# A selective-scan layer on one core: half of a GpSimd product, a mask product, a gate job, a low-part copy and a carry handover move to other tiles

## The reference, cut to what matters

```python
xr, gate = split(x @ W_in.T, 2)              # x: 2 sequences x 2048 steps x 512
xr = xr + t_emb
xc = silu(causal_conv4(xr) + b_conv)         # depthwise, 1024 channels
xn = layernorm(xc) * ln_g + ln_b
Bm, Cm, dt = split(xn @ W_xproj.T, 3)        # 16 states each
dt = tanh(dt @ W_dt.T + b_dt) * 0.01
Ad = 1.0 + dt * A
Bd = Bm * minimum(norm(xn), 1.0)
h  = clip(h * ad[:, :, None] + bd[:, :, None] * xt[:, None, :], -10, 10)   # scan over the steps
yt = einsum('bd,bdh->bh', ct, h)
y  = ys + D * xn                             # the "D product"
out = x + (y * silu(gate)) @ W_out.T
```

## Time and profile before

| | before |
|---|---|
| median of 3 executions | 2055.43 us (2054.57 to 2057.09) |
| profiled execution, its own time | 2052.24 us |
| span of the profiled execution | 2050.5 us |
| TensorE matmul busy | 1826.6 us, 89% |
| GpSimd busy | 1753.4 us, 86% |
| VectorE busy | 1637.6 us, 80% |
| ScalarE busy | 1376.2 us, 67% |

### The profile page before, as it was taken

How to read it: one execution, slowest core, us unless ns; L and a number is a source line. 1 busy time by engine, 2 the same in 40 slices (tenths; PEclk the granted TensorE clock), 3 DMA queues, 4 the chain that set the end, 5 groups by cost and what they waited for, 6 DMA issues and landing times.

```text
span 2050.5 us, 46002 instructions
## 1 busy us (share of the span) xinstructions
PE 1826.6 (89%) x16240; PEld 1396.0 (68%) x16240; DVE 1637.6 (80%) x2109; ACT 1376.2 (67%) x3462; POOL 1753.4 (86%) x1476
## 2 busy tenths in 40 slices
PE   5689998899999899999898999899999899899888
PEld 4466776676776676676676777676677676677655
DVE  3478887888887888888887888788888788888786
ACT  5577666777666776766676766676766677766643
POOL 1489988889988889988889988889988889988886
PEclk9799999999999999999999999999999999999999
DMA  5222222222222222222222222222222222222221
GB/s 178 58 69 54 70 58 74 63 78 59 67 58 75 62 79 59 67 57 77 62 77 59 67 63 71 62 75 59 69 72 62 64 73 61 67 75 58 62 67 29
DMA packets 168069, 139.14 MB, mean 68 GB/s; under 512 B 100704, under 2 KB 137968, under 8 KB 163168
## 3 DMA queue, kind: packets, MB, share of 16 engines
q1 hardware_dynamic: 167840, 136.20, 24.9%
HBM read 62.07 MB, written 9.31 MB: 35 GB/s over the span
## 4 chain that ended last, share of the span: by engine, by line
PE 29%; POOL 25%; issue 19%; ACT 15%; DVE 8%; SPq 2%; DMA 1%; POOLq 0%; DVEq 0%; ACTq 0%
POOL prod L1094 17%; PE ps_y L590 6%; ACT tap L750 5%; PE ps_job L517 5%; PE ps_job L483 4%; DVE ks L995 4%; PE ps_fill L573 3%; PE ps_fill L564 3%; ACT low L793 3%; PE ps_job L496 2%; POOL xn L1039 2%; POOL xn L1042 2%; PE ps_job L490 2%; SPq L406 1%; ACT xh L688 1%
## 5 line engine op out<-in xcount | busy, mean ns | idle before, releaser
L1094 POOL TENSOR_TENSOR prod<-ks,crep 128x512 f32<-128x512 f32 x1024 | 1286.0, 1274 | 142.1 <-DVE ks L995 140.4
L995 DVE TENSOR_TENSOR_SCAN ks<-low,ps_fill 128x512 f32<-128x512 f32 x1024 | 1208.3, 1208 | 227.0 <-PE ps_fill L573 226.7
L793 ACT COPY low<-ps_fill 128x512 f32<-128x512 f32 x1024 | 584.6, 580 | 477.0 <-PE ps_fill L564 474.4
L590 PE MATMUL ps_y<-c_sb,prod 128*128 128x128 f32 x4096 | 613.4, 275 | 9.9 <-ACT xc L758 7.1
L590 PEld LDWEIGHTS ps_y<-c_sb,prod 128*128 128x128 f32 x4096 | 457.5, 142 | 75.9 <-issue 27.1
L573 PE MATMUL ps_fill<-spans,pick 128*128 128x512 f16 x1024 | 390.7, 381 | 76.4 <-ACT low L793 71.8
L564 PEld LDWEIGHTS ps_fill<-ts,xs 128*128 128x128 f16 x4096 | 315.8, 98 | 171.8 <-issue 10.7
L564 PE MATMUL ps_fill<-ts,xs 128*128 128x128 f16 x4096 | 397.9, 220 | 9.2 <-DMA xs<-h 7.6
L750 ACT ACTIVATE tap<-xr,cols_sb 128x128 f32<-128x128 f32 x768 | 251.9, 393 | 0.0
L478 PE MATMUL ps_job<-x,w_in 128*128 128x128 f16 x3072 | 215.9, 221 | 10.3 <-POOL x L1064 7.8
L483 PE MATMUL ps_job<-w_in,x 128*128 128x512 f16 x768 | 202.0, 379 | 21.3 <-ACT gate L682 21.3
(11 more groups left out here) (124 smaller groups left out, 1962.7 us busy)
## 6 DMA issues: line engine op xcount, KB each, us to landing
crep<-c_dram SPq DMA_DIRECT2D x32, 1024.0 KB, 4.7
xs<-xh SPq DMA_DIRECT2D x256, 64.0 KB, 2.0
xs<-xl SPq DMA_DIRECT2D x224, 64.0 KB, 2.0
xf<-in_xT SPq DMA_DIRECT2D x32, 256.0 KB, 2.8
res<-in_x SPq DMA_DIRECT2D x32, 256.0 KB, 2.8
out_dram<-res SPq DMA_DIRECT2D x32, 256.0 KB, 2.3
ts<-tth SPq DMA_DIRECT2D x128, 32.0 KB
ts<-tth SPq DMA_DIRECT2D x128, 31.0 KB
```

The lines of the kernel that those rows point to most:

```text
L590: last = mm(ps_y[:, cut], prod[:, (TILES * k + s) % HOLD, e, :], ident, start=False, stop=(u % 4 == 3 and q == 3 and e == QN - 1), is_tran ...
L793: copy(low[:, (TILES * k + s) % RING], ps_fill[:, (TILES * k + s) % RING]).then_inc(sem["low_copied"], 1)
L995: nc.vector.tensor_tensor_scan(ks[:, u % 2, QN * q:QN * (q + 1)].rearrange("d n t -> d (n t)"), low[:, g % RING], ps_fill[:, g % RING], 0. ...
L1094: tt(prod[:, g % HOLD], ks[:, u % 2, part], crep[:, p, part], ALU.mult).then_inc(sem["weighed"], 1)
```

## The change

Six things move; no arithmetic is added or taken out.
1. The second gate job goes from points 8 to 11 to points 9 to 12, and its take from 12 to 13.
2. The second half of the D product goes from tile 11 to tile 22, with the wait for the transposed y of the chunk before.
3. The second mask product (`ttl`) goes from tile 18 to tile 21.
4. `bqm`'s low part goes from point 27 to 29.
5. In the carries ScalarE makes the fp16 copy at TAKE and copies the 16 rows into `lend` one point later, behind a wait for VectorE's low part; VectorE no longer waits for `lend_set`. The bank of a carry counts as free at `lend_set`.
6. The taps move from points 24, 28, 30, 34, 38, 40, 43, 46 to 24, 28, 33, 38, 40, 42, 44, 47.

```diff
-                (7, 1, "yT", 1, -1, 2, 1), (8, 4, "gate", 1, 0, 2, 0),
+                (7, 1, "yT", 1, -1, 2, 1), (9, 4, "gate", 1, 0, 2, 0),
...
-        TAKE = {("z", 0): 5, ("gate", 0): 7, ("hend", 0): 6, ("yT", 1): 8, ("gate", 1): 12,
+        TAKE = {("z", 0): 5, ("gate", 0): 7, ("hend", 0): 6, ("yT", 1): 8, ("gate", 1): 13,
...
-        TAP_AT = [24, 28, 30, 34, 38, 40, 43, 46]
+        TAP_AT = [24, 28, 33, 38, 40, 42, 44, 47]
...
-                    pe.wait_ge(sem[name + "_taken"], (kk + off) * per + i + 1)
+                    freed = "lend_set" if name == "carry" else name + "_taken"
+                    pe.wait_ge(sem[freed], (kk + off) * per + i + 1)
...
                     copy(ch[:, half], bank("carry", i)).then_inc(sem["carry16"], 1)
+                for i in range(2):
+                    if point != TAKE["carry", i] + 1 or not exists(k, 1):
+                        continue
+                    half = slice(i * BANK, (i + 1) * BANK)
+                    act.wait_ge(sem["carry_taken"], 2 * (k + 1) + i + 1)
                     if exists(k, 0):
                         act.wait_ge(sem[f"lend_in{p}"], 16 * pair(k, p, 0))
                     copy(lend[:, half], bank("carry", i)[0:NS]).then_inc(sem["lend_set"], 1)
-                if point == 27 and exists(k, 1):
+                if point == 29 and exists(k, 1):
...
-                    dve.wait_ge(sem["lend_set"], 2 * j + i + 1)
...
                         pool.wait_ge(sem["xn_done"], k + 1)
+                        skipped(p, 0)
+                    if s == 22 and exists(k, 0):
                         since(pool, "yT_in1", N_YT * k)
-                        for i in range(2):
-                            half = slice(i * BANK, (i + 1) * BANK)
-                            tt(xd[i], xn[:, p, half], row_d[:, half], ALU.mult).then_inc(sem["xd_done"], 1)
+                        skipped(p, 1)
...
-                    if s in (14, 18) and exists(k, 1):
-                        h = s // 4 - 3
+                    if s in (14, 21) and exists(k, 1):
+                        h = s // 21
...
+            def skipped(p, i):
+
+                half = slice(i * BANK, (i + 1) * BANK)
+                tt(xd[i], xn[:, p, half], row_d[:, half], ALU.mult).then_inc(sem["xd_done"], 1)
```

## The result

The changed kernel takes 2126.24 us (median of four executions, 2120.06 to 2130.53) against 2055.0 us for the kernel before (median of four; the 2055.43 above is that of three): the ratio is 1.0346, 95% interval 1.0317 to 1.0375. Forecast were 2115 us, 2080 to 2136.

A forecast was written before the change was run, and what follows sets the result against it. No engine alone was the bound; the copies behind `ttl` would bind. Waits of 53.7 (steady), 3.9 and 2.4 us, together 60, on 2052.24 make 2112; the median, 3.2 above, gives 2115 us, range 2080 to 2136.

The forecast's parts named there:

- The chain from `ttl` to the fill: GpSimd's `ttl`, SyncE's 18 copies, then the next chunk's tile 0 fill: 15.1 us to the landing, 2.5 us of room.
- `ttl` 5.2 us later, 2.7 over the room: At tile 21 `ttl` ends 5.2 us later; with 2.5 us of room the fill waits 2.7 us a pass, less G.
- The sum: 29 steady passes at 1.85 us make 53.7, pass 0 adds 3.9 and pass 30 adds 2.4: together 60 us.
- G: How much earlier the other moves bring the scan of tile 21: 0.25 (gate) + 0.6 (carries) = 0.85 us a pass.
- D product worth nothing in a steady pass: Moving its second half takes 1.27 us from GpSimd's full stretch before tile 21, but gains nothing in a steady pass.
- The taps cost nothing here: First conv take comes about 0.8 us later, but TensorE awaits it ahead of a fill already late: no cost.
- The page's 2.0 us: Fixed cost of a DMA; by it room is 4.0 us, the wait 1.2 less G, some 10 us over 29 passes.
- The three waits: The waits that the edits name, 1.77, 2.21 and 0.78 us; the faster rival had them go nearly in full.
- the faster one: Rival: scan of tile 21 over 2.7 us earlier, copies land in time, pass 0.55 us shorter, 2038 us; chance 0.05.
- The rival that ScalarE is the bound: Copies not the bound; the late conv take costs 0.8 - 0.25 = 0.55 us a pass, 2072 us; chance 0.03.

The follow-up runs named there:

- `ttl` back: The changed kernel with the second mask product (`ttl`) back at tile 18, every other move kept: 2057.82 us, ratio 1.0019.
- `ttl` alone: The kernel before with the second mask product (`ttl`) moved to tile 21 and nothing else: 2192.58 us, ratio 1.0676.
- the wait split: The changed kernel, all moves kept, but SyncE issues the eight copies of `tth` before waiting for `ttl`: 2058.29 us, ratio 1.0027.

## Why the prediction was right, and where it was off

- **The chain from `ttl` to the fill**, with its room read from the landing of the last copy: right, and shown by three runs (`ttl` back, `ttl` alone, the wait split).
- **`ttl` 5.2 us later, 2.7 over the room.** Right in kind, 0.5 us too small in this pass. From the end of `ttl` to the fill I counted 15.1 us, the time to the landing; the fill of the pass shown starts 1104.64 - 1088.97 = 15.67 us after it. Some 0.25 us of that lie between the landing and the matmul, the rest in the copies: three carry copies took 3.08 us to issue there (1.85 before), and the last copy landed 2.5 us after its issue instead of 3.5.
- **The sum.** The steady pass shown is 5.2 - 2.5 + 0.5 - 1.07 = 2.1 us longer in place of 1.85. By the fills' times, pass 0 lost 152.26 - 148.78 = 3.5 us (forecast 3.9), the 29 steady passes (1991.91 - 152.26) - (1926.98 - 148.78) = 61.5 (forecast 53.7) and pass 30 (2052.15 - 1991.91) - (1985.02 - 1926.98) = 2.2 (forecast 2.4). The profiled execution came out 8 us over its forecast of 2112, and the steady passes are where the sum was short. The other 3 of the 11 us are the step to the median: it stands 6.2 us above the profiled execution, not 3.2.
- **G.** 0.85 forecast, 1.07 measured. Its parts stand in the table: gate 0.24 (forecast 0.25), `bqm` 0.71, handover 0.11. For the last two together I forecast 0.6: the size was about right, the attribution wasn't. I had put the gain of the second low part down to the removed `lend` copy, and it came from `bqm`. In time the handover alone is worth nothing.
- **The clock** was no term of the sum. In the changed kernel it fell behind two of the 29 steady fills, from 661 to 665 us and from 1548 to 1552 us, after waits of 2.32 us (which the profile puts down to a scan) and 1.62 us. The passes there are together 3.7 us longer than the others, which is nearly half of the 8 us. With `ttl` alone the clock was a third of the loss (46 of 140).
- **D product worth nothing in a steady pass**: right (61.00 us with and without); over the whole no gain is shown.
- **The taps cost nothing here.** True only because TensorE was late at the fill anyway. I counted the sets ahead of the conv take (seven in both) and not those between the y cast's wait and the take. Once the copies no longer bind, the new tap points cost 18.5 us, and the handover on top 18 more. The take comes 49.81 - 49.41 = 0.4 us later, where I had 0.8.
- **The page's 2.0 us.** The Trainium skill (DMA: Bandwidth & Descriptors, section "Anatomy of one DMA") gives this figure for DMAs issued by GpSimd, and the prediction left that out; SyncE issues the copies here. They landed after 2.5 to 3.5 us, and the 10 us worked out from the page's figure stand against 71 measured.
- **Rivals.** The three waits did not go in full, against the faster one. The rival that ScalarE is the bound came out once `ttl` was put back, at 2058 instead of the 2072 given: the pass then takes 0.36 us more than before, not 0.55.

## What to carry to other kernels

Before an operation is moved to a later place because its own engine has time there, follow its output into the DMA queue: the room is the time from the landing of the last transfer behind that wait to the instruction that needs it, not the idle time of any engine. In an in-order queue split a wait, so that transfers whose data is ready don't stand behind one whose data isn't. And when a wait names the last of several instructions of a busy engine, removing that instruction from the wait only renames it; what helps is filling an idle gap ahead of the busy stretch, as `bqm` did. To find what sets a steady pass, measure several events from one fixed point in a few variants: the one that keeps its distance to the end of the pass is it.

## What the runs showed of the hardware

A regular wait of about 3 us at one place of a 65 us pass lowered TensorE's granted clock behind it in 28 of 29 steady passes, and so cost half as much again as the wait itself (94 us more of waits, 140 us of time). Waits of 1.3 to 1.7 us at the same place did so once in 28, and one of 2.32 us did as well. Behind the 2.32 us wait the granted clock was 0.60 from 661 to 663 us, 0.55 from 663 to 665 and full again after that.

The executions of the changed kernel spread over 10 us, those of the kernel before over 5. The changed kernel's four go with their mean clock: 2120.06, 2125.53, 2126.96 and 2130.53 us at 0.983, 0.982, 0.980 and 0.978. Whether the clock or the copies' landings (2.5 us after the issue in the pass shown, 2.5 and 3.5 in that of before) make the spread is not shown, since only one of the four was profiled.
